# GpSimd instead of VectorE adds the MLP's last bias to the residual

## The reference

```
h1 = n1_w * arcsinh(h) + n1_b
h  = h + proj(attention over the 3 x 3 neighbourhood, 8 heads, q k v from h1)
h2 = n2_w * arcsinh(h) + n2_b
ff = gelu(h2 @ mlp_w1 + mlp_b1) @ mlp_w2 + mlp_b2
return h + ff
```

## Time and profile before

| | |
|---|---|
| median of 3 runs | 4216.26 us (4207.89 to 4223.81) |
| profiled execution | 4228.25 us, of it 4226.5 us span |
| busy share of the span | PE 95%, DVE 86%, ACT 86%, POOL 86% |
| bands | 128, so some 33 us per band with the opening and the end |

### The profile page before, as it was taken

How to read it: one execution, slowest core, us unless ns; L and a number is a source line. 1 busy time by engine, 2 the same in 40 slices (tenths; PEclk the granted TensorE clock), 3 DMA queues, 4 the chain that set the end, 5 groups by cost and what they waited for, 6 DMA issues and landing times.

```text
span 4226.5 us, 123614 instructions
## 1 busy us (share of the span) xinstructions
PE 4022.6 (95%) x47688; PEld 2518.8 (60%) x47688; DVE 3637.2 (86%) x6174; ACT 3630.9 (86%) x5377; POOL 3636.9 (86%) x4092
## 2 busy tenths in 40 slices
PE   5899999999999999999999999999999999999997
PEld 3566556655666656566666666666656666656664
DVE  5888888888889888888888898888888888888884
ACT  4888888888888888889888888888888888988884
POOL 2788888888889888889988898898888898888885
PEclk8999999999999999999999999999999999999998
DMA  4555555555555555555555555555555555555551
GB/s 120 134 145 148 139 145 146 144 143 143 145 147 147 143 146 139 146 144 147 148 144 147 147 142 151 143 145 148 141 147 147 144 147 145 147 146 142 149 133 55
DMA packets 511562, 598.83 MB, mean 142 GB/s; under 512 B 76799, under 2 KB 409601, under 8 KB 508417
## 3 DMA queue, kind: packets, MB, share of 16 engines
q1 hardware_dynamic: 510976, 590.93, 53.1%
HBM read 197.30 MB, written 135.40 MB: 79 GB/s over the span
## 4 chain that ended last, share of the span: by engine, by line
PE 46%; SPq 18%; DMA 14%; POOL 9%; issue 7%; ACT 4%; DVE 2%; POOLq 0%; ACTq 0%; DVEq 0%
PE ps L368 46%; SPq L325 14%; DMA v_win<-v_rows 8%; DMA v_rows<-v_nat 6%; POOL p_lo L1065 3%; POOL g_lo L1091 2%; SPq L306 2%; DVE v_nat L766 1%; SPq L292 1%; POOL g_hi L1089 1%; POOL a_lo L1073 1%; ACT ln_s L920 1%; POOL a_hi L1071 1%; ACT p_hi L981 1%; ACT v_nat L966 1%
## 5 line engine op out<-in xcount | busy, mean ns | idle before, releaser
L1065 POOL TENSOR_TENSOR p_lo<-prob,p_hi 100x512 f16<-100x512 f32 x1024 | 1322.2, 1301 | 392.7 <-ACT p_hi L981 391.8
L980 ACT ACTIVATE prob<-ps 100x512 f32<-100x512 f32 x1024 | 613.3, 599 | 269.0 <-PE ps L368 267.6
L368 PEld LDWEIGHTS ps<-v_win,p_hi 100*128 100x128 f16 x8192 | 464.6, 98 | 396.9 <-DMA v_win<-v_rows 185.6
L368 PE MATMUL ps<-v_win,p_hi 100*128 100x65 f16 x8192 | 516.8, 194 | 150.3 <-DMA v_win<-v_rows 114.3
L1091 POOL TENSOR_TENSOR g_lo<-g,g_hi 128x512 f16<-128x512 f32 x512 | 600.8, 1173 | 41.0
L807 DVE TENSOR_TENSOR o_norm<-ps,recip 64x128 f32<-64x128 f32 x2048 | 591.3, 289 | 49.4
L981 ACT ACTIVATE p_hi<-ps 100x512 f16<-100x512 f32 x1024 | 617.0, 603 | 0.0
L791 DVE TENSOR_REDUCE maxima<-ps 128x8 bf16<-128x800 f32 x512 | 507.9, 992 | 50.2 <-PE ps L368 35.5
L706 DVE TENSOR_TENSOR ln_u<-ln_u,ln_s 128x1024 f32<-128x1024 f32 x256 | 367.5, 1435 | 162.5 <-ACT ln_s L911 158.7
L368 PE MATMUL ps<-v_win,p_lo 100*128 100x65 f16 x4096 | 481.9, 193 | 0.0
L988 ACT ACTIVATE g<-ps,b 128x512 f32<-128x512 f32 x512 | 338.5, 686 | 147.7 <-PE ps L368 146.2
(11 more groups left out here) (91 smaller groups left out, 10844.2 us busy)
## 6 DMA issues: line engine op xcount, KB each, us to landing
keys<-k_win SPq DMA_DIRECT2D x1536, 100.0 KB, 2.4
v_win<-v_rows SPq DMA_DIRECT2D x1024, 101.6 KB
queries<-q_nat SPq DMA_DIRECT2D x1536, 64.0 KB
v_rows<-v_nat SPq DMA_DIRECT2D x256, 260.0 KB, 4.5
xT<-in_x_dram SPq DMA_DIRECT2D x128, 512.0 KB, 4.0
out_dram<-y SPq DMA_DIRECT2D x256, 256.0 KB, 3.2
queries<-in_query_mask_dram SPq DMA_DIRECT2D x128, 160.0 KB
keys<-in_mlp_w_dram SPq DMA_DIRECT2D x2, 512.0 KB, 7.6
```

The source lines that it names most:

```text
L368: return pe.matmul(o, a, b, start=start, stop=stop, skip_group_check=True)
L980: act.activation(prob[b][0:NK], ps[0:NK, B_ST + b, :], ACT.Exp, scale=INV * INV).then_inc(prob_ready, 1)
L1065: pool.tensor_tensor(p_lo[b][0:NK], prob[b][0:NK], p_hi[b][0:NK], ALU.subtract).then_inc(p_lo_ready, 1)
```

## The change

The function `h_plus_bias`, which adds `b2` to both channel groups of `h` (two instructions, 128 x 512 fp32, in place), moves from VectorE's program to GpSimd's. On VectorE it stood in quarter 1 of a step, on GpSimd it stands in quarter 2, behind the second `g_parts`. Its semaphore is renamed. Nothing else is changed.

```diff
-            def h_plus_bias(t, par):
-                v.wait_ge(asinh2, signals(t, 1, 1))
-                for g in range(G):
-                    v.tensor_scalar(h[par][:, g, :], h[par][:, g, :], b2[:, g:g + 1], None, ALU.add).then_inc(hb_ready, 1)
...
-                    if k == 1 and fin:
-                        h_plus_bias(t - 2, par)
...
+            def h_plus_bias(t, par):
+                pool.wait_ge(asinh2, signals(t, 1, 1))
+                for g in range(G):
+                    pool.tensor_scalar(h[par][:, g, :], h[par][:, g, :], b2[:, g:g + 1], None, ALU.add).then_inc(hb_ready, 1)
...
                     if k == 2 and fin:
                         g_parts(t - 2, (2, 3))
+                        h_plus_bias(t - 2, par)
```

More of the change, by code:

```diff
@@ L188, in build @@
         pe_s, pe_st, pe_av, pe_ot = (sem("pe_" + s) for s in ("s", "st", "av", "ot"))
-        h_ready, hb_ready, abs1, abs2, sum1, sum2 = (sem("dve_" + s) for s in ("h", "hb", "abs1", "abs2", "sum1", "sum2"))
+        h_ready, abs1, abs2, sum1, sum2 = (sem("dve_" + s) for s in ("h", "abs1", "abs2", "sum1", "sum2"))
         asinh1, asinh2, y_ready = (sem("dve_" + s) for s in ("asinh1", "asinh2", "y"))
@@ L203, in build @@
         win_main = sem("act_win_main")
+        hb_ready = sem("pool_hb")
         win_bottom, win_top = sem("pool_win_bottom"), sem("pool_win_top")
```

## The result

The changed kernel takes 4486.27 us (median of 4 runs, 4483.39 to 4488.31) against 4214.68 us (4 runs, 4207.89 to 4223.81): ratio 1.0647, 95% interval 1.063 to 1.0665. It is 272 us slower, 2.1 us for each of the 128 bands. The forecast was 4229 us, its range ended at 4300.

A forecast was written before the change was run, and what follows sets the result against it. Each step's start was taken as the later of the gather transfer (109 bands) and GpSimd's chain (19). 0 us gained on VectorE and 12.7 us lost on GpSimd, on the 4216.26 us median, gave 4229 us, range 4206 to 4300.

The forecast's parts named there:

- T: Duration of one bias addition on GpSimd, taken as 0.68 us, near the cast `a_hi`.
- D: Delay of GpSimd's later work up to the next step's tile 0: 2T - 0.96 us, 0.40 us for T = 0.68.
- rival 1: The addition on GpSimd costs like a two-input instruction, 1.1 us or more: 4300 us; chance 0.30.
- VectorE's relief: Two additions of 1.0 us per band leave VectorE, which then waits for ScalarE instead: worth 0 us.
- The room ahead of tiles 6 and 7: GpSimd's idle time ahead of `p_lo` of these tiles, 0.86 us, absorbs part of the two additions.
- the longest slack assumed: GpSimd's slack in the 109 bands where the transfer is last, estimated as even from 0 to 1.72 us.
- Rival 2: Relieving VectorE does count: TensorE's waits for `o_norm`, 24.8 us, would go, giving 4191 us; chance 0.08.
- rival 3: All is hidden: T near 0.6, covered by the transfer's arrival, 4216 + 7 us or less; within the 0.62 of the likeliest case.
- The slower case: The whole kernel becomes slower: chance 0.32, against 0.60 for same and 0.08 for faster.
- the likeliest case: GpSimd's addition takes between 0.6 and 0.77 us, giving 4216 to 4237 us; chance 0.62.

The follow-up runs named there:

- The four forms: Changed kernel with four 128 x 256 instructions (two tensor_scalar, a copy, a tensor_tensor) in the bias's place on GpSimd: 4350.68 us in its only run.
- `sum2` moved: Changed kernel with VectorE's `sum2` put behind the normalisation of tile 6: 4392.96 us (4391.65 to 4396.76).

## Why the prediction was wrong

**The step that failed: the bounds of T.** The prediction bounded the unknown addition by the cast (0.61 us) and the two-tensor subtraction (1.16 us), as one tensor input seemed to put it between them, and took 0.68. It is 1.56 us, which makes D 2.17 us instead of 0.40. The four forms show that the number of inputs is not what orders them: copy 397, tensor_tensor 611, tensor_scalar 848 to 922 ns at 256 elements. The nearest rows by shape were no bound. An operation that the trace of that engine didn't show should have kept an open upper end, and rival 1 with it.

**The frame held.** VectorE's relief was put at 0 us: 0.9995 without the bias. The room ahead of tiles 6 and 7 and D = 2T - 0.96 gave steps of 32.4 us for T = 1.04 (measured 32.41) and 33.46 us for T = 1.56 (measured 33.42, once nothing else stood in the way). The whole: with D = 2.17 us, beyond the longest slack assumed, 19 x 2.17 + 109 x (2.17 - 0.86) = 184 us, against 4393 - 4215 = 178 us with `sum2` moved, the slack and the 4215 us being those of the first chip. On the chip of that experiment, where the transfers leave the kernel before at 4252 us, its loss is 141 us. So on the first chip about two thirds of the loss are this one term with the wrong T.

**What the sum lacked: 93 us.** The prediction saw that `p_lo` of tile 7 moves towards `sum2`, had `sum2` late by up to 0.4 us and counted nothing. With additions of 3.1 us it is `p_lo` of tile 6, the one that TensorE waits for, that starts just behind `sum2`. The wait there, 1.71 us without the hold-up, becomes 2.64 us; the prediction had it at 0.1 us and inside D. That makes the step 33.75 us instead of 33.42, 0.33 x 126 = 42 us over the steps that have both an MLP and an attention. And in some steps TensorE's clock falls within this wait, which costs 35.08 - 33.75 = 1.33 us in the one shown; the 33 long steps of the trace are together 47 us above 33.75 us each. The groups of `g` matmuls bear this out over the run (busy us, mean ns, of the changed kernel):

```profile
L369 PE MATMUL ps<-g_hi,w_hi 128*128 128x512 f16 x1024 | 407.9, 398 | 5.4 <-POOL g_lo L1085 5.2
L369 PE MATMUL ps<-g_lo,w_hi 128*128 128x512 f16 x1024 | 406.3, 397 | 0.0
...
L369 PE MATMUL ps<-g_hi,w_lo 128*128 128x512 f16 x1024 | 402.3, 393 | 0.0
```

In the kernel before they were 391.2, 389.1 and 389.3 us, and with `sum2` moved 391.3, 389.3 and 389.0; the sum is 47 us more. 42 + 47 is 89 of the 93 us. The split between the two is worked out from the trace; the experiment took both away together, and no run has the one without the other.

**The rivals.** Rival 1 came nearest: it had the place of the loss and the sign, with too small a price; its T ended at 1.2 us. Its reason, that the addition costs like a two-input instruction, does not hold either, as those took 1.04 and 1.16 us. Its signs came (T above 0.8 us, the wait for `v_win` gone), except that tile 6 and not the step's opening is where TensorE waits; SyncE's wait for `v_low`, said to stay, went from 124 to 341 us. Rival 2 is refuted by the run without the bias, and so is rival 3 by the 272 us. The slower case had 0.32, the likeliest case 0.62, so the chances leaned the wrong way as well.

By the Trainium skill, "GPSIMD Engine Reference", section "Engine selection", elementwise work belongs on VectorE, and one-input work runs on GpSimd at roughly line rate. The first agrees with the 272 us lost; the second does not hold for this instruction, which took 1564 ns on GpSimd and 480 at least, 831 in the median, on VectorE. The measurement decides.

**Of the reading before:** that the transfer's arrival opened most steps was right, but SyncE's list was close behind it, and I had not priced it. The page of the kernel before shows it in the shares of the chain that ended last:

```profile
PE 46%; SPq 18%; DMA 14%; POOL 9%; issue 7%; ACT 4%; DVE 2%; POOLq 0%; ACTq 0%; DVEq 0%
```

SyncE's queue (SPq) has twice GpSimd's share of that chain.

## What to carry to other kernels

Moving work to an engine that shows no such instruction in its trace has no upper bound from rows of the same shape: measure that one form first, since on GpSimd the choice of instruction for the same sum was worth 211 of 272 us here. Read the slack where the work is put, not the busy share: GpSimd's 86% hid 0.86 us of room in the quarter that mattered, and VectorE's 2 us per band were worth nothing. When a list shifts, check which instruction is then held up by the other engine, and read TensorE's granted clock in each new wait; these two made a third of the loss.

## What the runs showed of the hardware that I had not expected

- GpSimd: tensor_scalar 1564 ns at 128 x 512 fp32 (922 ns at 256; 848 ns with an immediate), tensor_tensor with one operand broadcast 1040 ns (611 at 256), copy 397 ns at 256.
- After the same wait of 2.64 us TensorE's matmuls took 6.21 us in one step, with a granted clock of 0.50, and 4.88 us in the next; 33 of the steps were of the first kind. The run's mean clock was 0.979; with the wait of 1.71 us of the sum2 experiment it was 0.993.
- Moving 256 instructions changed others that stayed where they were: VectorE's pass over `h` took 781 instead of 1626 ns, and `sum2` holds up whichever GpSimd instruction starts beside it, `a_hi` (1.61 instead of 0.61 us), `p_lo` (the pair 3.20 instead of 2.27) or `a_lo` (2.04 instead of 1.16).
- The kernel before took 4215 us on one chip and 4252 to 4255 us on others; the changed kernel, which doesn't wait for transfers, took 4486 us on the first and 4480 us, with one semaphore more, on another.
